# Start-up pieces as ordered steps, own order for the first and the last batch, attention product in 32-column tiles: a transformer block on one Trainium2 core

## The reference

```python
xn = _layernorm(x, axis=-1)
x = x + _L0_attn_ref(xn, ...) + _L0_ffn_ref(xn, ...)

# _L0_attn_ref
q, k, v = qkv[:, :, 0], qkv[:, :, 1], qkv[:, :, 2]      # xn @ W_qkv
q, k = rotary_embedding(q, ...), rotary_embedding(k, ...)
scores = jnp.where(mask, q k^T / sqrt(64), NEG_INF)
out = jnp.einsum('bhqk,bkhd->bqhd', softmax(scores), v)
return out @ W_out

# _L0_ffn_ref
x = x + layernorm(softmax(q k^T / sqrt(8)) v @ Wo + bo, g1, be1)
gate_probs = jax.nn.softmax(x @ Wg + bg, axis=-1)
top_vals, top_idx = jax.lax.top_k(gate_probs, 2)
all_out = jnp.einsum('bsd,edf->bsef', x, We) + bexp
return x + layernorm(sum of top_vals * picked all_out, g2, be2)
```

## Time and profile before

| | |
|---|---|
| runs | 1297.58, 1302.23, 1294.76 us (median 1297.58) |
| profiled execution, its own time | 1300.52 us |
| its span in the profile | 1298.7 us |
| PE busy | 1172.0 us, 90% |
| DVE busy | 939.6 us, 72% |
| ACT busy | 890.1 us, 69% |
| POOL busy | 815.1 us, 63% |
| granted TensorE clock, mean | 0.967 of full speed |

### The profile page before, as it was taken

One profiled execution on the slowest core, in us unless ns is written; L12 is line 12 of the kernel. 1 busy time (PEld: TensorE's weight loads), 2 busy tenths in 40 slices (PEclk: granted clock), 3 DMA queues, 4 the chain that ended last, 5 costly groups with the idle time before them and its releaser, 6 DMA issues.

```text
span 1298.7 us, 26053 instructions
## 1 busy us (share of the span) xinstructions
PE 1172.0 (90%) x8393; PEld 757.8 (58%) x8393; DVE 939.6 (72%) x2328; ACT 890.1 (69%) x1840; POOL 815.1 (63%) x733
## 2 busy tenths in 40 slices
PE   4789989999999999989899898989999899999995
PEld 2355656556575665655666465655657456575564
DVE  7657587966878487875879758796587965779555
ACT  3578776686758877568766677657776686667871
POOL 2765784677747784467844678455775566556752
PEclk8899999999999999989999899998999989899998
DMA  4000100011001010010100110001000011001100
GB/s 140 33 34 25 42 25 21 30 50 42 17 33 34 34 41 18 25 34 34 42 17 26 41 42 25 21 22 50 34 30 21 17 42 42 17 25 34 40 11 9
DMA packets 33962, 42.92 MB, mean 33 GB/s; under 512 B 5536, under 2 KB 17060, under 8 KB 33832
## 3 DMA queue, kind: packets, MB, share of 16 engines
q1 hardware_dynamic: 30360, 38.31, 8.5%
q10 hardware_dynamic: 3472, 2.95, 0.7%
HBM read 5.60 MB, written 2.10 MB: 6 GB/s over the span
## 4 chain that ended last, share of the span: by engine, by line
PE 53%; ACT 17%; DVE 16%; issue 11%; POOL 1%; DMA 1%; SPq 0%; ACTq 0%; DVEq 0%; POOLq 0%
PE work L1053 8%; ACT pn L666 7%; PE work L1065 6%; PE work L964 6%; PE work L1118 6%; PE work L1038 5%; ACT fpt L622 5%; PE work L1081 5%; PE work L966 4%; PE work L965 4%; DVE fnmax L816 4%; PE work L1090 4%; PE work L1107 3%; DVE branch L901 2%; DVE work L898 2%
## 5 line engine op out<-in xcount | busy, mean ns | idle before, releaser
L816 DVE TENSOR_REDUCE fnmax<-work 128x2 f32<-128x1024 f32 x256 | 303.4, 1220 | 115.9 <-PE work L1090 114.8
L524 POOL TENSOR_TENSOR raw<-raw,cos_t 128x512 f32<-128x512 f32 x128 | 164.0, 1281 | 292.3 <-DMA swapped<-raw 288.0
L666 ACT ACTIVATE pn<-work,nmax 128x512 f32<-128x512 f32 (+3 forms) x512 | 265.0, 540 | 94.4 <-DVE nmax L916 94.0
L622 ACT ACTIVATE fpt<-work 128x1024 f32<-128x1024 f32 x256 | 251.3, 1033 | 74.5 <-PE work L1107 72.6
L916 DVE CUSTOM_DVE_ANT_0 work<-work,causal 128x512 f32<-128x512 f32 (+3 forms) x512 | 236.1, 521 | 74.5 <-PE work L1038 73.2
L1053 PE MATMUL work<-consts,pn 128*128 128x128 f32 x1280 | 174.0, 282 | 3.0 <-ACT pn L666 1.1
L528 POOL TENSOR_TENSOR raw<-raw,swapped 128x512 f32<-128x512 f32 x128 | 163.4, 1276 | 10.0
L1053 PEld LDWEIGHTS work<-consts,pn 128*128 128x128 f32 x1280 | 146.6, 144 | 36.6 <-DVE fnmax L816 12.5
L539 POOL TENSOR_TENSOR qk_l<-raw,qk_h 128x512 fp32r<-128x512 f32 x128 | 162.8, 1279 | 3.8
L525 POOL TENSOR_TENSOR swapped<-swapped,sin_t 128x512 f32<-128x512 f32 x128 | 163.8, 1279 | 0.0
L675 ACT COPY pt<-work 128x1024 f32<-128x1024 f32 x128 | 128.8, 1014 | 38.3 <-PE work L1053 38.0
(11 more groups left out here) (152 smaller groups left out, 2210.9 us busy)
## 6 DMA issues: line engine op xcount, KB each, us to landing
swapped<-raw SPq DMA_DIRECT2D x256, 128.0 KB, 2.0
x_in<-in_L_attn_x_dram SPq DMA_DIRECT2D x8, 256.0 KB, 3.1
out_dram<-x_in SPq DMA_DIRECT2D x8, 256.0 KB, 2.5
fpt<-in_L_attn_W_qkv_dram ACTq DMA_DIRECT2D x3, 512.0 KB, 6.0
pt<-in_L_ffn_We_dram ACTq DMA_DIRECT2D x1, 512.0 KB, 6.9
wout<-in_L_attn_W_out_dram ACTq DMA_DIRECT2D x1, 512.0 KB, 8.2
pt<-in_rope_dram ACTq DMA_DIRECT2D x1, 192.0 KB, 4.1
affine<-in_L_ffn_g_dram SPq DMA_DIRECT2D x2, 64.0 KB, 4.0
```

What stands on the lines that cost most here:

```text
L524: nc.gpsimd.tensor_tensor(raw[:, n % 3], raw[:, n % 3], cos_t[:], ALU.mult)
L622: nc.scalar.activation(fpt[:, ((b * G + g) * T + i) % FP, 2 * r:2 * r + 2].rearrange("p h n -> p (h n)"), bank_of(("fst", b, g, i), 2 * r, 2),
L666: ins = nc.scalar.activation(pn[:, h, PN_AT[j]:PN_AT[j] + n], bank_of(("sc", b, c, unit), h)[:, at:at + n], ACT.Exp, scale=-1.0, bias=nmax ...
L816: nc.vector.tensor_reduce(fnmax[:, j, 2 * r:2 * r + 2, 0:1], bank_of(("fsm", b, g, j), 2 * r, 2).rearrange("p (f n) -> p f n", f=2), AX.X, ...
```

## The change

**The prologue becomes steps.** Fourteen kinds are new and occur once: turn, tt, tab (rotary tables on DVE, PE, ACT), str, strl (strips for fqk), tb, qkb (bias columns), wh and wl (three parts of W_qkv, high and low), smh, sml, bia, weh, wel (the small weights, the biases, the experts). Each has a number in START, a semaphore of its own, and its readers in batch 0 wait for that in place of `prepared`. The loads of W_qkv's first two parts are issued ahead of the rotary table, the third behind the small weights. ACT runs one exponential on a spare tile ahead of everything else. Waits for some loads and cleared tiles are separate (columns_loaded, causal_loaded, cleared_bias, cleared_psum).

**Orders.** All numbers in START, SHIFT and PSUM are new, and with FIRST and LAST every single step of batch 0 and batch 7 has its own shift. SHIFT holds only batches 1 and 6. The order changes somewhat on all engines.

**The product.** pv runs as four matmuls of 32 columns for each key tile in place of two of 64.

The diff, cut: of the tables only a few lines stand here, since a number says nothing without the others.

```diff
+ONCE = ("turn", "tt", "tab", "str", "strl", "tb", "qkb", "wh", "wl", "smh", "sml", "bia", "weh", "wel")
...
+LOADED = ("tt", "strl", "tb", "sml", "bia", "wel")
...
-    "rs2": [80.952],
+    "rs2": [72.205001],
...
-PERIOD = 159.4702
+PERIOD = 159.4553
...
-    "fqkl": {0: 1.664, 6: 0.203, 7: 0.538},
...
+def later(kind, b, n):
+    own = {0: FIRST, B - 1: LAST}.get(b, {}).get(kind)
+    return own[n] if own else SHIFT.get(kind, {}).get(b, 0)
...
-TIME = {(kind, b) + key: PERIOD * b + at + SHIFT.get(kind, {}).get(b, 0) for kind in START
-        for b in range(B) for key, at in zip(KEYS[kind], START[kind])}
+TIME = {(kind, b) + key: PERIOD * b + at + later(kind, b, n) for kind in START
+        for b in range(1 if kind in ONCE else B) for n, (key, at) in enumerate(zip(KEYS[kind], START[kind]))}
...
         def _(act):
             NQ = H * DH
+            for n in range(2):
+                act.dma_start(raw_qkv[:, n * NQ:(n + 1) * NQ], w_qkv[:, n * NQ:(n + 1) * NQ]).then_inc(wqkv_loaded[n], 16)
             act.dma_start(angles, rope.rearrange("(t p) c -> p t c", p=P)).then_inc(rope_loaded, 16)
-            for n in range(3):
-                act.dma_start(raw_qkv[:, n * NQ:(n + 1) * NQ], w_qkv[:, n * NQ:(n + 1) * NQ]).then_inc(wqkv_loaded[n], 16)
...
+            act.dma_start(raw_qkv[:, 2 * NQ:3 * NQ], w_qkv[:, 2 * NQ:3 * NQ]).then_inc(wqkv_loaded[2], 16)
...
+            act.wait_ge(cleared, 1)
+            nc.scalar.activation(warm[:], warm[:], ACT.Exp)
...
                     act.wait_ge(*after("fst", b, g, i))
                     if b == 0:
-                        act.wait_ge(prepared, 1)
+                        for n in range(3):
+                            act.wait_ge(*after("wl", 0, n))
...
                 elif kind == "xl":
                     dve.wait_ge(*after("xh", b))
                     nc.vector.tensor_tensor(xt_l[:, b % 2], bank_of(("xT", b)), xt_h[:, b % 2].bitcast(F32), ALU.subtract).then_inc(done["xl"], 1)
-                    if b == 0:
-                        rest_of(0)
-                        rest_of(1)
-                        other_weights()
...
                     if g == 0:
                         pe.wait_ge(*after("xl", b))
-                        pe.wait_ge(strips_ready, 6)
+                        if b == 0:
+                            pe.wait_ge(*after("strl", 0))
...
                     for i in range(T):
-                        for h in range(2):
-                            ins = nc.tensor.matmul(psum[h * DH:(h + 1) * DH, i * P:S], v[:, i, 2 * c + h],
+                        for a in range(0, 2 * DH, STRIP):
+                            h = a // DH
+                            ins = nc.tensor.matmul(psum[a:a + STRIP, i * P:S], v[:, i, 2 * c + h, a % DH:a % DH + STRIP],
                                                    pt[:, c % 2, h, PT_AT[i]:PT_AT[i] + S - i * P],
-                                                   start=i == 0, stop=i == T - 1, tile_position=(0, h * DH))
+                                                   start=i == 0, stop=i == T - 1, tile_position=(0, a))
```

More of the change, by code:

```diff
@@ new lines @@
+    "ln1": [67.256823],
+    "rs1": [24.295537],
+    "nm1": [70.443051],
+    "x2": [32.349857],
+    "x2T": [-43.019359],
+    "x2h": [111.083105],
+    "x2l": [80.435659],
+    "gate": [-31.104177],
+    "gsub": [84.421221],
+    "gexp": [125.82449],
+    "pick": [86.248502],
+    "moe": [-25.100661, -11.407106, -7.912755, -7.236805],
+    "moew": [90.035884, 92.307012, 92.341107, 92.709171],
+    "res": [54.592557],
+    "ln2": [99.090519],
+    "rs2": [72.205001],
+    "nm2": [105.021664],
@@ new lines @@
+    "gsub": {1: 0.376729, 6: -0.785494},
+    "gexp": {1: -2.977722, 6: -5.499358},
+    "pick": {1: -0.240224, 6: -1.756548},
+    "moe": {1: 0.517056},
+    "moew": {1: -0.038045},
+    "res": {1: -12.139758, 6: 84.572927},
+    "ln2": {1: -1.175023},
+    "rs2": {1: 14.334498, 6: -0.18637},
+    "nm2": {1: 1.172911, 6: 1.463171},
+    "out": {1: -5.124839, 6: 90.790774},
+    "store": {1: -16.864741, 6: 177.808467},
+    "proj": {6: 0.000406},
+    "raw": {1: 0.080745, 6: -0.093914},
+    "swap": {1: -6.410637, 6: -4.188564},
@@ L752, in _ @@
[L752 removed]
+            nc.vector.memset(work[:], 0.0).then_inc(cleared_psum, 1)
+            dve.wait_ge(cleared_psum, 1)
             links = [0]
```

672 lines of the change are left out of this document (414 added, 258 removed), and 81 rows, old and new, of tables (FIRST, LAST, PSUM, SHIFT).

## The result

| | before | after |
|---|---|---|
| median of the runs | 1298.18 us (4 runs) | 1283.11 us (4 runs, 1279.87 to 1283.32) |
| ratio to before, 95% interval | | 0.9888 (0.9847 to 0.993) |
| profiled execution, its own time | 1300.52 us | 1279.87 us |
| its span | 1298.7 us | 1277.9 us |

The change makes the kernel 1.1% faster. (The profiled execution is the fastest of its four runs, 3.2 us under the median.) The forecast was 1263 us, 2.7%: the sign was right, the time lies near the upper end of the range, and less than half of the forecast gain came. The kernel before varies more from run to run than the changed one: in the series of the experiments its runs went from 1289.09 to 1300.41 us, so its profiled execution, at 1300.52, lies at the slow end. By spans the gain is 20.8 us, by the medians of this table 15.1, and in the second series (experiment 3) 10.7.

What follows compares the result with a forecast made beforehand. PE, busy 1172.0 of 1298.7 us, was taken as bound, delayed by DVE's collisions with POOL. 1298.7 − 33.4 − 3 − 4 + 4 = 1262.3 us span, 1264.1 with 1.8 above it; less 2.9 for the median, 1263 taken; range 1248 to 1286.

Steps and rivals of the forecast that it cites:

- The cause of the long batches: Middle batches: xn and nm2 on DVE wait for POOL's work bunched behind rs2; moving rs2 gives −33.4 us over six steps.
- fqkl(7,1): Batch 7, DVE: it stands behind an ffn maximum, costing some 6 us of idle and half clock; counted inside the −33.4.
- The tiles: Attention product in 32-column tiles: fewer changes of tile shape on PE, −3 us, between −5 and 0.
- weight loads in the open: Rival, main attention's 64 products: 16 further loads each aren't hidden, +72 to +143 us, 1335 to 1405; chance 0.04.
- the start, −4: New prologue: fqkl(0,0) ends 2.7 us earlier, later steps better packed, −4 us by the first gate row; bounds 0 and −8.
- a first gate row later than 211.9: Sign of being wrong: batch 0's gate exponential on ACT starting later than 211.9 us.
- The end, +4: Batch 7: PE waits some 3 us for ch and cl, res slows nm2, an ACT wait goes: net +4, bounds −3 to +10.
- the collision moves: Rival: some slow places stay or new orders open waits of 2 to 4 us with half clock, 1278 to 1290; chance 0.14.
- The term for the median: Runs' median against the profiled execution: 1297.58 lies 2.9 us below 1300.52, so −2.9 us was carried over.

Runs made afterwards that it cites:

- experiment 3: Changed kernel with 64-column tiles: 1287.74 us; unedited again: 1283.06 us; kernel before with experiment 1's edit and 32-column tiles: 1267.42 us.
- experiment 1: Kernel before with only rs2 of batches 2 to 5 moved later on POOL, behind rope(4,0) and hi(3,1): 1266.06 us, ratio 0.9807.
- experiment 2: Changed kernel with rs2 of batches 1 to 5 put back ahead of rope(3,1) on POOL: 1299.28 us in a single run.
- experiment 7: Kernel before with experiment 1's edit, 32-column tiles, and rs2(6), xn(7) and batch 7's fqkl placed as in other batches: 1265.65 us, ratio 0.9792.
- experiment 6: Kernel before with experiment 1's edit, 32-column tiles and the new prologue, its pieces placed into the old order: 1268.65 us, ratio 0.9802.
- experiment 4: Changed kernel with only xn(1) on DVE moved behind max(0,2,2,1): 1278.69 us, ratio 0.9889.
- experiment 5: Changed kernel, batch 7's cT, ch, cl, res moved: 1288.65 us; other places and free PSUM banks: 1277.22; the latter plus experiment 4's edit: 1274.08.

## Why the prediction was right in the middle and wrong at the ends

- **The cause of the long batches** was right: xn and nm2 against POOL's bunched work behind rs2 (experiments 1 and 2, and nm1 as the control). Six steps gave −36.7 us where −33.4 and some 2.3 for the tiles (6/8 of 3) were forecast.
- **fqkl(7,1)** was named as a loss of its own of some 6 us, 1.5 of wait and the rest of the clock. With its place kept and only rs2 moved, the wait stayed (1.73 us) and the half clock went (experiment 1), so its own part is about the wait. Its repair, together with those of nm2(6) and xn(7), took 1.7 us off the last full step (experiment 7). Since it stood inside the −33.4, the sum wasn't hurt.
- **The tiles**: −3 was forecast, −3 was measured in the new order, 0 in the old one. The fear of weight loads in the open didn't come true. On PE's timelines of the changed kernel, matmuls and four loads in their midst:

```profile
708.24 2.36 PE L1280 MATMUL work<-pt,v 128*32 128x512 f32 x32
...
708.69 0.13 PEld L1280 LDWEIGHTS work<-pt,v 128*32 128x32 f32 x4 [0.30 <-issue]
```

  The product takes 2.36 us with 32 loads, as 2.38 with 16 in the earlier trace rows; that rival, with a chance of 0.04, is out. The rule of the Trainium skill, "TensorE: Matmul & The Clock Gate", section "Part 3: Packing small matmuls — row/col tiling", by which loads overlap only with matmuls of another row group, doesn't hold for this kernel's column tiles.
- **The step that failed: the start, −4, was +7.9.** Two things in it. The first is size: the walk through the prologue was right up to fqkl(0,0) (21.7 forecast, 21.3 measured), but "with later steps better packed" was an assumption, and the lead of 2.9 us is 0.6 at the first score product. In experiment 6, in another order, it shrank to 0.3 by there. The second is the larger: the forecast looked for collisions at nm2 and at xn of the middle batches and said that xn may meet POOL at no cost, from one place where nothing behind it was late. For xn(1) in batch 0's own order nothing was looked up. There inv(0,1) stands behind it, and PE waits 3.10 us. Experiment 4 gives 3 to 4 of the 12 us to this. The forecast's bounds for the start, 0 and −8, had no loss in them at all, and "a first gate row later than 211.9" was its own sign of being wrong; it came, at 219.80.
- **What of the start stays open**: with xn(1) repaired, gate 0 is still at 216 to 217 us, and at 210.3 in the order of before (experiment 3). The prologue isn't the reason (experiment 6), so it is the new order of batch 0. The windows from the first score product to gate 0, experiment 4's kernel first, then experiment 3's in the order of before:

```profile
56.00:216.78 160.78, 146.75 (x1199) 91.88 (x1199) 108.17 (x264) 121.89 (x253) 101.38 (x90) 0.98 0.08 28
...
56.36:210.28 153.92, 140.95 (x1181) 88.35 (x1180) 106.14 (x263) 119.38 (x251) 99.17 (x88) 1.00 0.08 29
```

  Of the 6.9 us between them PE is idle for only 1.1 and busy for 5.8. Two stretches of 3.4 us at half clock, near 80 and 186 us, where the other kernel has none, account for some 3.4 of these (an estimate, half their length); the rest is in part work that the new order puts ahead of this row (18 instructions more). The first stretch follows a wait of 2.04 us for fexp. No experiment took these places away. A version of the changed kernel with the steady order for the later part of batch 0 wasn't tried on the chip.
- **The end, +4, was +8.0.** The places were right (cT and wo behind the last scores, res under nm2: nm2(7) 2.05 us, 1.11 without), the cause of PE's waits only in part: ahead of cT it was a PSUM bank and not the chain; ahead of wo a bank too, but cl came only 0.2 us sooner. A bank doesn't show in the order of instructions; it stands in the PSUM table, which wasn't followed through at this place. The half clock behind the two waits (3.4 us) wasn't in the sum either, only in the upper bound of +10, which held. Experiment 5 shows the banks, with the chain's steps moved in the same edit; it can't give each its share.
- **The range** held the time by 3 us, and that was luck: its upper end stood for slow places left in the middle, and none was. The ends lost 16 us against the sum. Nearest to what happened came the rival "the collision moves", with a chance of 0.14 and 1278 to 1290 us: it named new waits of 2 to 4 us with half clock behind them, from changed orders of DVE and ACT, and the 3.10 us at 94.58 is one; but it looked for them in the batches of the middle.
- **The term for the median**, −2.9, was +3.2: the changed kernel's profiled execution was the fastest of its four and not one of the slow ones. Of the 20 us between 1263 and 1283, 15.6 are span, 6.1 are this term, 0.2 the time above the span, and −1.8 that 1263 was taken where the sum by this term gives 1261.2.
- The statement that start and end can differ from the sum by −7 to +10 doesn't follow from their bounds, which give −11 to +10. They differed by +15.9.

## What to carry to other kernels

Where one engine's instruction gets slow, list every place of it and what stands behind it at each, and do this for the new order too: the same instruction at the same length was nearly free in one place (xn(7) in experiment 1, 4.28 us, in a step of 151.0) and cost a wait of 3 us with a clock drop behind it in another (xn(1), 4.31). Before a large reordering is credited or blamed, try the smallest edit that touches the suspected cause alone; here one number for four batches gave more than the whole change. A wait of PE that an exponential ends may be a wait for a PSUM bank: read the bank table along with the order. And look at how far the runs of the kernel before lie apart before its one profile is made the base of a sum.

## What the runs showed of the hardware

- A DVE tensor_scalar from SBUF to SBUF is held up by POOL's work on SBUF: 1.06 to 1.12 us for four alone, up to 4.47 together in the kernel before and 4.72 in experiment 2's. From PSUM to SBUF, in the one place under POOL's work and in the seven without, four take 1.36.
- Going from a product in two column tiles to one in four costs PE some 0.12 us; between groups of equal shape it is gone (2.30 against 2.17 us, and 0.98 against 0.86 for the second block's product ahead of it). The number of weight loads, 16 or 32 in a product, makes no difference that shows (2.38 and 2.36 us).
- Idle times of PE of 1.31 and 1.73 us were followed by a stretch of 6.8 us at 1.2 GHz (1235.00 to 1241.80). The same place doesn't always give one: behind the same wait of 1.06 to 1.07 us, in the same order, one kernel had 6.8 us at 1.2 GHz and the other none (experiment 5). In two executions of the changed kernel the stretches between 38 and 58 us were one of some 17 us and two of some 6.8; the spans are 1280.9 and 1277.9 us.
